# Top layers in four sets with tiles of their own, and form 0 of the left factor by DMA and ScalarE

## The reference

```python
e = stack([tbl_m[ids[:, m]] for m in range(32)], axis=1)      # (512, 32, 16)
x0 = xk = e
for W in (W0, W1, W2):                                          # (32, h, 64); h = 32, 64, 64
    xk = relu(einsum('bmd,bhd,mhk->bkd', x0, xk, W))
    outs.append(sum(xk, axis=2))                                # (512, 64)
h = concatenate(outs + [dense_ctx], axis=1)                     # (512, 192 + 16)
h = maximum(h @ W_top1 + b_top1, 0)                             # 512 wide
h = maximum(h @ W_top2 + b_top2, 0)                             # 256 wide
y = h @ W_top3                                                  # (512, 1)
```

## Time and profile before

| | |
|---|---|
| median of 3 runs | 353.35 us |
| the profiled execution: time, span | 353.74 us, 351.9 us |
| PE busy, records | 305.4 us (87%), 1476 |
| DVE busy, instructions | 274.2 us (78%), 173 |
| POOL busy, instructions | 254.2 us (72%), 193 |
| ACT busy, instructions | 61.6 us (18%), 122 |
| DMA | 52.07 MB; share of 16 engines: SyncE's queue 34.2%, ScalarE's 11.5%, POOL's 3.0% |

### The profile page before, as it was taken

One profiled execution on the slowest core, in us unless ns is written; L12 is line 12 of the kernel. 1 busy time (PEld: TensorE's weight loads), 2 busy tenths in 40 slices (PEclk: granted clock), 3 DMA queues, 4 the chain that ended last, 5 costly groups with the idle time before them and its releaser, 6 DMA issues. The chain is left out here.

```text
span 351.9 us, 3914 instructions
## 1 busy us (share of the span) xinstructions
PE 305.4 (87%) x1476; PEld 112.7 (32%) x1476; DVE 274.2 (78%) x173; ACT 61.6 (18%) x122; POOL 254.2 (72%) x193
## 2 busy tenths in 40 slices
PE   0016859798999988999999999999999999998986
PEld 0013513243334222323333333233333334333426
DVE  0024949799999969999999999999999788954201
ACT  1001210301220330012201220222031104113011
POOL 5775678879788988888898879898919567917000
PEclk9999996999999999999999999999999999999998
DMA  5374956957973984286338643952580102100000
GB/s 178 45 251 83 369 111 180 376 88 213 381 149 65 279 329 80 28 337 260 56 71 303 272 72 77 378 190 61 151 327 0 45 2 63 45 2 0 0 0 0
DMA packets 52282, 52.07 MB, mean 148 GB/s; under 512 B 37574, under 2 KB 42568, under 8 KB 49064
## 3 DMA queue, kind: packets, MB, share of 16 engines
q1 hardware_dynamic: 41272, 39.92, 34.2%
q10 hardware_dynamic: 6896, 10.85, 11.5%
q0 software_dynamic: 4096, 1.06, 3.0%
HBM read 41.33 MB, written 2.10 MB: 123 GB/s over the span
## 5 line engine op out<-in xcount | busy, mean ns | idle before, releaser
L519 DVE TENSOR_TENSOR z_vector<-left,r_forms 128x2048 f32<-128x2048 f32 (+3 forms) x140 | 260.0, 1924 | 45.4 <-DMA r_forms<-x_rows 23.0
L569 PE MATMUL result<-z_vector,w_sb 128*64 128x512 f32 (+2 forms) x1056 | 213.9, 557 | 41.5 <-DVE z_vector L519 40.2
L309 POOL DMA_INDIRECT gathered_rows<-table,row_index x128 | 121.8, 951 | 41.2 <-issue 34.5
L324 POOL TENSOR_TENSOR z_pool<-r_forms,xj_forms 128x1024 f32<-128x1024 f32 (+2 forms) x60 | 131.8, 2232 | 24.7 <-PE result L569 15.0
L569 PEld LDWEIGHTS result<-z_vector,w_sb 128*64 128x64 f32 x1056 | 77.3, 142 | 172.9 <-issue 143.4
L569 PE MATMUL result<-z_pool,w_sb 128*64 128x512 f32 (+2 forms) x240 | 51.8, 571 | 0.0
L384 ACT ACTIVATE x_sb<-result 128x512 f32<-128x512 f32 (+2 forms) x27 | 14.9, 551 | 169.7 <-PE result L569 169.7
L499 DVE TENSOR_REDUCE d_sums<-x_sb 128x32 f32<-128x512 f32 (+2 forms) x27 | 16.8, 625 | 20.0 <-ACT x_sb L384 20.0
L569 PEld LDWEIGHTS result<-z_pool,w_sb 128*64 128x64 f32 x240 | 15.7, 136 | 34.1 <-issue 33.2
L368 ACT ACTIVATE left<-xj_forms 128x512 f32<-128x512 f32 (+2 forms) x36 | 18.6, 547 | 17.1 <-DMA xj_forms<-x_sb 6.8
L359 ACT ACTIVATE left<-h_form 128x512 f32<-128x512 f32 (+2 forms) x18 | 10.0, 553 | 59.8 <-DVE z_vector L519 44.9
(11 more groups left out here) (32 smaller groups left out, 28.1 us busy)
## 6 DMA issues: line engine op xcount, KB each, us to landing
r_forms<-x_rows SPq DMA_DIRECT2D x24, 1024.0 KB, 10.4
r_forms<-x_rows SPq DMA_DIRECT2D x8, 768.0 KB, 6.8
xj_forms<-x_sb ACTq DMA_DIRECT2D x24, 256.0 KB, 4.0
h_form<-x_rows SPq DMA_DIRECT2D x12, 256.0 KB, 3.0
gathered_rows<-table,row_index POOLq DMA_INDIRECT x128, 3.3
r_forms<-x_rows SPq DMA_DIRECT2D x4, 512.0 KB, 6.1
x_rows<-gathered_rows SPq DMA_DIRECT2D x24, 64.0 KB, 2.5
xj_forms<-x_sb ACTq DMA_DIRECT2D x8, 192.0 KB, 3.1
```

The lines of the kernel that those rows point to most:

```text
L309: nc.gpsimd.indirect_dma_start(gathered_rows[:, half % GATHERED, g], None, table, bass.IndirectOffsetOnAxis(ap=row_index[:, at:at + 1], ax ...
L324: nc.gpsimd.tensor_tensor(z_pool[:, unit % NZP, t, :, 0:columns(p)], r_form(q, p, t)[:, s0:s1], xj1_forms[form_buffer(n, p)][:, t, 0:colum ...
L519: nc.vector.tensor_tensor(z_vector[:, unit % NV, t, 0:s1 - s0, 0:columns(p)], left[:, t, bank, 0:columns(p)].unsqueeze(1).broadcast_to([12 ...
L569: done = nc.tensor.matmul(result[n][K * t:K * t + K, 0:columns(p)], weights, z[:, t, 0:columns(p)], start=first, stop=last)
```

## The change

- `SAMPLES` is 16, 16, then seven times 32, so the last pair has 32 samples, not 24, and pair 1 has 16.
- `select` and its matrix go. `load_xj0(n, p)` spreads maps 0 to 31 of x with two DMAs on ScalarE's queue into a single SBUF tile `xj0_form`; `copy_xj0(n, p)` copies it to `left` bank 0 when the second unit of the layer before it is through on VectorE. VectorE and POOL wait for `left0_copied` where they waited for `selected`.
- Top layers run in four sets of 64 samples of each half (128 columns), with tiles of their own: top 1 of set 0 in stage (2, 3), top 2 in (1, 5), top 3 after (0, 6); of set 1 two pairs later; set 2 from (1, 8) on; the last set at the end, except that its first top 1 half (layers 0 and 1 of the network) is done within (2, 8). Outputs of each set are stored by DMA from ScalarE's queue.
- Squares are made in place in `h_form`, so SyncE loads it again when TensorE has used them. `table_base` goes. The room for POOL's gather descriptors is `dynamic_dma_scratch_size=4096`, was 8192.

```diff
-SAMPLES = [16, 24] + [32] * 6 + [24]
+SAMPLES = [16, 16] + [32] * 7
...
+GROUP_ENDS = [3, 5, 7, 9]
+TOP1_AT = [4, 6]
+GS = B // 8
+GC = 2 * GS
...
                     sp.wait_ge(left_copied, left_copies((0, p - 1), t))
-                    sp.wait_ge(z_square_ready, 2 * (p - 1) + t + 1)
+                    sp.wait_ge(z_square_used, p)
                 sp.dma_start(h_form[:, t, 0:columns(p)],
...
-            pool.wait_ge(selected, 1)
+            pool.wait_ge(left0_copied, 2)
...
-                    if p > 0:
-                        act.wait_ge(z_square_used, p)
-                    nc.scalar.activation(z_square[:, t, 0:columns(p)], h_rows, ACT.Square).then_inc(z_square_ready, 1)
+                    act.wait_ge(left_copied, left_copies((0, p), t))
+                    nc.scalar.activation(h_rows, h_rows, ACT.Square).then_inc(z_square_ready, 1)
...
                             act.wait_ge(xj1_loaded[n][t], 16 * p)
+                            act.wait_ge(xj0_loaded[t], 16 * (LAYER_AT[n + 1, p - 1] + 1))
                 nc.scalar.activation(x_sb[n][:, 0:columns(p)], result[n][:, 0:columns(p)], ACT.Relu).then_inc(x_ready[n], 1)
+            def load_xj0(n, p):
+                at = LAYER_AT[n, p]
+                act.wait_ge(x_ready[n - 1], p + 1)
+                if at > 0:
+                    act.wait_ge(left0_copied, 2 * at)
+                for t in range(2):
+                    rows = x_sb[n - 1][K * t:K * t + H, 0:columns(p)]
+                    act.dma_start(xj0_form[:, t, 0:columns(p)], rows.unsqueeze(1).broadcast_to([H, DELTAS, columns(p)])
+                                  ).then_inc(xj0_loaded[t], 16)
+            def copy_xj0(n, p):
+                at = LAYER_AT[n, p]
+                for t in range(2):
+                    act.wait_ge(xj0_loaded[t], 16 * (at + 1))
+                    if at > 0:
+                        act.wait_ge(z_vector_ready, 2 * VECTOR_BEFORE[LAYERS[at - 1]] + 3 + t)
+                    nc.scalar.activation(left[:, t, 0, 0:columns(p)], xj0_form[:, t, 0:columns(p)], ACT.Copy
+                                         ).then_inc(left0_copied, 1)
             def load_xj1(n, p):
...
+            def load_dense(group):
+                if group > 0:
+                    act.wait_ge(top1_summed, group)
+                act.dma_start(top_in[K:K + D, 1], dense[:, :, samples(group)]).then_inc(dense_loaded, 16)
...
+            def top_inputs(group, layers):
+                for n in layers:
+                    act.wait_ge(x_summed[n], GROUP_ENDS[group])
                     for t in range(2):
...
+                        top_block(n, t, group, top_in_ready)
+            def top_hidden1(group):
+                act.wait_ge(top1_summed, group + 1)
+                for k in range(N1):
+                    nc.scalar.activation(hidden1[:, k], top1_psum[k], ACT.Relu,
+                                         bias=b_top1_sb[:, k:k + 1]).then_inc(hidden1_ready, 1)
...
+            def top_out(group, y):
+                if group > 0:
+                    act.wait_ge(y_stored, 16 * group)
+                nc.scalar.activation(y_sb[:], y, ACT.Copy).then_inc(y_ready, 1)
+                act.wait_ge(y_ready, group + 1)
+                act.dma_start(out.rearrange("(t b) o -> o t b", t=2)[:, :, samples(group)],
+                              y_sb[:].rearrange("o (t b) -> o t b", t=2)).then_inc(y_stored, 16)
...
             copy_h(0)
             relu(0, 0)
+            load_xj0(1, 0)
             load_xj1(1, 0)
+            copy_xj0(1, 0)
             for p in range(NP - 1):
                 copy_xj1(1, p)
+                if p > 0:
+                    copy_xj0(2, p - 1)
                 copy_h(p + 1)
+                if p - 1 in TOP1_AT:
+                    top_hidden2(TOP1_AT.index(p - 1))
                 relu(1, p)
                 if p == 2:
                     load_top()
                 if p > 0:
                     copy_xj1(2, p - 1)
                 relu(0, p + 1)
+                load_xj0(1, p + 1)
                 load_xj1(1, p + 1)
+                copy_xj0(1, p + 1)
+                load_xj0(2, p)
+                if p in TOP1_AT:
+                    group = TOP1_AT.index(p)
+                    load_dense(group)
+                    top_inputs(group, range(3))
+                    top_hidden1(group)
+                if p - 1 in TOP1_AT:
+                    group = TOP1_AT.index(p - 1)
+                    act.wait_ge(top3_summed, group + 1)
+                    top_out(group, top3_psum)
                 if p > 0:
                     relu(2, p - 1)
                 load_xj1(2, p)
             last = NP - 1
             copy_xj1(1, last)
...
+            copy_xj0(2, last - 1)
+            third, fourth = 2, 3
+            load_dense(third)
+            top_inputs(third, range(3))
             copy_xj1(2, last - 1)
             relu(1, last)
+            load_xj0(2, last)
             load_xj1(2, last)
-            act.wait_ge(top_loaded, 16 * 7)
-            for k in range(N1):
-                early(k)
+            top_hidden1(third)
+            copy_xj0(2, last)
             copy_xj1(2, last)
-            for n in range(2):
-                act.wait_ge(x_summed[n], NP)
-                for t in range(2):
-                    top_block(n, t, (EARLY, NP), late_in_ready)
+            load_dense(fourth)
+            top_inputs(fourth, range(2))
+            top_hidden2(third)
             relu(2, last - 1)
-            for k in range(N1, N1 + N2 + 1):
-                early(k)
+            act.wait_ge(top3_summed, third + 1)
+            top_out(third, top3_psum)
             relu(2, last)
...
                     elif k == 0:
-                        dve.wait_ge(selected, LAYER_AT[n, p] + 1)
+                        dve.wait_ge(left0_copied, 2 * LAYER_AT[n, p] + t + 1)
...
+            def whole_top1(group):
+                pe.wait_ge(top_loaded, 16 * 6)
+                pe.wait_ge(dense_loaded, 16 * (group + 1))
+                pe.wait_ge(top_in_ready, 6 * (group + 1))
+                if group > 0:
+                    pe.wait_ge(y_ready, group)
+                top1(group)
...
+            def top3(group):
+                pe.wait_ge(hidden2_ready, N2 * (group + 1))
+                for m in range(N2):
+                    done = nc.tensor.matmul(top3_psum, w_top3_sb[:, m:m + 1], hidden2[:, m],
+                                            start=m == 0, stop=m == N2 - 1)
+                done.then_inc(top3_summed, 1)
+            def late_top1_begun():
+                pe.wait_ge(top_in_ready, 6 * (len(GROUP_ENDS) - 1) + 4)
+                pe.wait_ge(y_ready, len(GROUP_ENDS) - 1)
+                pe.wait_ge(x_ready[0], NP)
+                late_top1(0)
...
-            pe.wait_ge(select_loaded, 16)
-            select(1, 0)
             pe.wait_ge(w12_loaded, 16)
             for p in range(NP - 1):
-                layer(1, p, {1: [lambda: select(2, p - 1)]} if p > 0 else {})
+                made, ended = p in TOP1_AT, p - 1 in TOP1_AT
+                layer(1, p, {1: [lambda: top2(TOP1_AT.index(p - 1))]} if ended else {})
                 vector_unit(0, p + 1, 0)
                 squares(p + 1)
+                if ended:
+                    top3(TOP1_AT.index(p - 1))
                 if p > 0:
-                    layer(2, p - 1, {1: [lambda: select(1, p + 1)]})
-                else:
-                    select(1, 1)
+                    layer(2, p - 1, {"pool": [lambda: whole_top1(TOP1_AT.index(p))]} if made else {})
             last = NP - 1
-            layer(1, last, {1: [lambda: select(2, last - 1)]})
-            early(0)
-            layer(2, last - 1, {0: [lambda: early(1)], 1: [lambda: select(2, last), lambda: early(2)],
-                                "pool": [lambda: early(3)]})
-            layer(2, last, {0: [lambda: early(N1)], 1: [lambda: early(N1 + 1)], "pool": [lambda: early(N1 + N2)]})
-            pe.wait_ge(late_in_ready, 6)
+            layer(1, last)
+            whole_top1(2)
+            layer(2, last - 1, {1: [lambda: top2(2)]})
+            layer(2, last, {0: [lambda: top3(2)], "pool": [late_top1_begun]})
...
+            late_top1(1)
...
-    nc = bacc.Bacc("TRN2", target_bir_lowering=False, num_devices=1, dynamic_dma_scratch_size=8192)
+    nc = bacc.Bacc("TRN2", target_bir_lowering=False, num_devices=1, dynamic_dma_scratch_size=4096)
```

More of the change, by code:

```diff
@@ L112, in pool_after, with build @@
     return POOL_BEFORE[stage] + len(pool_units(*stage))
-def build(nc, table, ids, base, w0, w0_mirror, not_twice, w12, select, dense, w_top1, b_top1, w_top2, b_top2, w_top3,
-          out):
+def build(nc, table, ids, base, w0, w0_mirror, not_twice, w12, dense, w_top1, b_top1, w_top2, b_top2, w_top3, out):
     x0_dram = nc.dram_tensor("x0_rows", (NP, 2, ROWS * C), F32).ap()
@@ L290, in _ @@
                     load_r1(p, t)
-            for k, samples in enumerate((slice(0, START[EARLY]), slice(START[EARLY], B // 2))):
-                sp.wait_ge(y_ready, k + 1)
```

(38 more changed lines are left out.)

153 lines of the change are left out of this document (47 added, 106 removed).

## The result

The changed kernel takes 360.35 us (median of four runs, 358.75 to 360.47), the kernel before beside it 352.58 (351.65 to 353.98). The ratio is 1.021, with a 95% interval of 1.016 to 1.026. The forecast was 356.8 us in a range of 350 to 363. The profiled execution took 358.75 us, 1.6 under its median, with a span of 356.9, where the one of before took 353.74.

A forecast was written before the change was run, and what follows sets the result against it. POOL's gathers hold the start, VectorE bounds the middle, TensorE the end. The last product comes 3.8 us later (345.7 for 341.94), what follows saves 0.75: +3.0 on the profiled 353.74 gives 356.8 us, range 350 to 363.

The forecast's parts named there:

- POOL resumes: In the start, POOL's gathers go on at 34.4 us after waiting for form 0, 2.8 later than before (31.61).
- (1, 2) on POOL: In the start, POOL begins products of layer 1 on pair 2 at 84.3 us, not 78.48, 5.8 later.
- (0, 4) on VectorE: VectorE starts layer 0 on pair 4 4.7 us after 125.76, with that pair's rotated forms issued at 120.8.
- Top layers enter: In layer 2 on pair 3, TensorE waits 1.8 us for dense features and is full from there to the end.
- A top matmul: Each top-layer matmul of 128 columns on TensorE takes 0.29 us, with ends of 0.26 and 0.31.
- No gap after (1, 5): TensorE, idle before layer 1 on pair 5, has no idle time after it.
- The larger pair 8: In TensorE's full stretch, 8 of the 9 us gained from selections and gap are paid for pair 8's 32 samples.
- The tail: From the last product near 346 us, 9.2 us to the end of the span; 0.75 us less than before.
- The gap before 323.72: In the kernel before, TensorE has a gap from 320.57 to 323.72 because ScalarE came late; 3.1 us to gain.
- the start costs little: Rival: the clock doesn't fall or POOL's gap closes, shift 0 to 1.6 us, not 4.7; 350 to 354; chance 0.31.
- Faster: Rival: no start shift, top matmuls at 0.26, no dense wait, 348.5 us, if pair 4's forms issue by 116.1; chance 0.08.
- Form 0 late: Rival: form 0's transfer, slowed beside rotated forms, costs 4 us a cycle over two to five cycles: 361 to 375; chance 0.08.

The follow-up runs named there:

- dense early: Changed kernel with the old sample split and dense features asked for two to three layers earlier, on chip C: 348.75 us, 0.987 of the kernel before.
- old samples, again: Changed kernel with the old sample split (16, 24, six times 32, 24), second time, on chip C: 353.15 us, 0.997 of the kernel before.
- hybrid: Changed kernel with old split, early dense features, form 0 by selection matmuls up to layer 1 of pair 4, by DMA afterwards: 342.72 us, 0.972.
- old samples on chip B: Changed kernel with the old sample split (16, 24, six times 32, 24), first time: 362.40 us, 0.986 of the kernel before.
- samples only: Kernel before with only the samples changed to 16, 16, seven times 32, on chip A: 366.85 us, 1.008 of the kernel before.

## Why the prediction was right, and where by luck

The mechanism was the one forecast: start later, full stretch even. By its own steps, in the profile:

- **POOL resumes** (34.4 forecast) at 37.70. This step failed in size, by 3.3 us. It priced form 0 by the place where the form 1 copy stood. The second half was asked for at 31.54, 0.9 later than that copy had been (30.66), and took 5.47 us, where the form 1 transfers of 128 KB took 3.0 before and 3.1 after in the median. It ran beside 4 x 512 KB of rotated forms of pair 1, asked for from 31.64 on; before, they were asked for from 34.25. With the small pair 1 they are ready earlier, and the forecast left that out. With the old split on chip C, where they come behind the transfer again, the second half was copied at 33.88 and POOL resumed at 34.53; with dense early the transfer took 3.3 us. That the loads slow the transfer is read from these profiles and was not tested by itself. The 1.2 to 1.5 us that the next wait gives back were 1.1. From old samples, again:

```profile
33.88 0.39 ACT L394 ACTIVATE left<-xj_form 128x256 f32<-128x256 f32 x1 [0.64 <-DMA xj_form<-x_sb]
```

```profile
34.65 1.24 SPq L257 DMA_DIRECT2D r_forms<-x_rows  x2
```

- **(1, 2) on POOL** (84.3) at 87.61: that same 3.3 us. The clock after the long wait fell as forecast (16 records 2.05 us over 3.65; the forecast had 2.9 for the whole of (0, 2)).
- **(0, 4) on VectorE** (130.5) at 132.06. SyncE issued pair 4's forms 9.7 us later than before and not 4.7 (POOL's last gather for them ended 8.0 later, and took 1.6 more to land), but they took 6.2 us to land after their issue, in place of 9.65. I held this constant; 3.4 us of the miss came back there.
- **Top layers enter**: the wait for the dense features (1.8 us from 184.4) was 1.62, up to 188.05, and TensorE is full from there.
- **A top matmul** (0.29) takes 0.25, under the 0.26 of the forecast's lower end: with 58 of them 16.7 us forecast, 14.6 in the chain, 2.1 less.
- **No gap after (1, 5)**: wrong by 2.4 us: 1.11 at 260.09 on the dense features of the second set, which the sum had counted for the first set only, 0.49 at 251.9 behind VectorE, and 0.79 at 332.86 behind a relu.
- **The larger pair 8** (8.0 us): 7.0 between the two profiles (5.3, and 1.7 for two chunks fewer), 8.1 against old samples, again. The 165 chunks from 188.05 on took 143.7 us, for 142.8.
- **The tail** (9.2) was 8.1 from the relu at 348.78 to the end of the span, 10.0 before. The last set's sixteen records of the second top layer took 2.10 us and not the 3.23 of before, which the forecast had kept.
- **The gap before 323.72** (3.1 us, to be gained) was misread: it is a gap in the chain, which runs over ScalarE there, and not in TensorE's work. TensorE did two more chunks in it and was idle for 1.3 us:

```profile
320.48 1.94 PE L569 MATMUL result<-z_vector,w_sb 128*64 128x512 f32 x8
323.72 2.80 PE L569 MATMUL result<-z_vector,w_sb 128*64 128x384 f32 x16 [1.31 <-ACT x_sb L384]
```

The forecast's check of the old stretch (116.6 for 116.3) came out all the same, since it priced the four chunks of 384 columns in such a row at 0.65 us each and they took 0.70. The 345.7 do not use this gap.

356.8 + 1.9 (TensorE takes over at 188.05 for 186.2) + 2.4 (gaps) - 2.1 (top matmuls) + 0.9 (price of the chunks) - 1.1 (tail) = 358.8, for 358.75. Five errors of 0.9 to 2.4 us stood partly against each other; that the sum came within 2 us is in part luck. What the forecast did not see at all is that medians and profiles differ in opposite ways (353.74 over 352.58, 358.75 under 360.35), which adds 2.8 us to the measured loss.

Of the rivals, "the start costs little" fell: the clock did fall and POOL stayed late. "Faster" fell on its own condition: pair 4's forms were issued at 125.82, not by 116.1. The hybrid shows what its start is worth with the old split and early dense features: 342.7. "Form 0 late" fell: VectorE waited for a copy of it twice after 100 us, 2.85 us at 115.24 (ahead of a wait for the rotated forms, at 132.06) and 1.12 at 319.76, and the stretch from (0, 4) on is 0.5 us longer than before. "Descriptor room" fell: gathers stand 1.25 us apart as before. The chance of 0.43 for no change was high because the forecast's own centre lay on that border; the terms that it missed went both ways.

## What to carry to other kernels

Work taken from an engine is worth something only in the stretch in which that engine sets the pace; work moved between pieces changes stretch with them. Ask of each half of a change in which stretch it lands, and make it there alone: here the same edit lost 6 to 8 us in the start and saved TensorE 9.7 at the end. A small transfer that releases a queue of gathers is priced beside the traffic that it starts among, not from its median (5.47 us here, for 3.0). A gap in the chain of waits is not idle time of the engine: look at the engine's own rows.

## What the runs showed of the hardware

On two chips the kernel before took 364 us; in the first measurement and on chip C it took 353. In the profiles of the slower ones TensorE stands still before single matmuls with nothing that ends the wait, here with the old samples on chip B:

```profile
50.32 1.44 PE L605 MATMUL result<-z_vector,w_sb 128*64 128x384 f32 x4 [1.38 <-DVE z_vector L556]
52.39 0.48 PE L605 MATMUL result<-z_vector,w_sb 128*64 128x384 f32 x1 [0.62 <-issue]
53.09 0.54 PE L605 MATMUL result<-z_vector,w_sb 128*64 128x384 f32 x2 [0.22 <-issue]
53.82 0.48 PE L605 MATMUL result<-z_vector,w_sb 128*64 128x384 f32 x1 [0.18 <-issue]
```

and ScalarE waits 16 to 28 us in all, in two to five places, marked "remote". In the two rows of samples only the signals come 8 and 10 us after the records of TensorE's matmuls. None of the four profiles on chip C nor the first two of this case has such a "remote" wait. It looks as if TensorE received its instructions late there; that was not shown, and what makes a chip so is open. It means that a price of the start from one chip does not hold on another: (0, 4) started at 132 on the one and at 139 on the other, in the same code.
